# Who copies a chunk's tokens and who adds the halves of its output: a cross-attention and mixture-of-experts kernel

## The reference, cut to what matters

```
x = x + attention(layernorm(x), ctx, ctx)         # x: 2 x 1024 x 256, float32
h = layernorm(x)                                  # 2048 tokens of 256
shared = (silu(h @ sg) * (h @ su)) @ sd           # hidden width 512
logits = h @ gate_w                               # 32 experts
e, top = argmax(logits), max(logits)
xs = h * sigmoid(top)                             # one expert per token
routed = (silu(xs @ G[e]) * (xs @ U[e])) @ D[e]   # G, U: 32 x 256 x 512, D: 32 x 512 x 256
x = x + shared + routed
```

## Time and profile before

| what | value |
|---|---|
| median of 3 runs | 293.36 us (292.28 to 294.63) |
| profiled execution | 291.1 us |
| its span | 289.2 us |
| mean granted clock of TensorE | 0.972 |
| busy: PE, DVE, ACT, POOL | 250.5, 163.1, 94.0, 87.9 us |
| HBM read, written | 59.49 MB, 8.91 MB |

### The profile page before, as it was taken

How to read it: one execution, slowest core, us unless ns; L and a number is a source line. 1 busy time by engine, 2 the same in 40 slices (tenths; PEclk the granted TensorE clock), 3 DMA queues, 4 the chain that set the end, 5 groups by cost and what they waited for, 6 DMA issues and landing times.

```text
span 289.2 us, 12925 instructions
## 1 busy us (share of the span) xinstructions
PE 250.5 (87%) x4627; PEld 184.6 (64%) x4629; DVE 163.1 (56%) x490; ACT 94.0 (33%) x284; POOL 87.9 (30%) x248
## 2 busy tenths in 40 slices
PE   4997899997799899998979999999999999698800
PEld 3765666553375358856867888788788787543700
DVE  0655796878469543016656667666666667424333
ACT  2344875454230110235323333334333333211000
POOL 1262221111005777102222223222222222103772
PEclk9996899999999999999999999999999999999985
DMA  6999994000001325401998869999999999733565
GB/s 196 328 394 410 404 401 157 2 2 1 2 0 37 109 96 165 160 16 50 329 390 286 300 236 331 358 410 415 416 410 411 415 412 409 312 83 94 174 214 164
DMA packets 32559, 68.69 MB, mean 238 GB/s; under 512 B 3966, under 2 KB 18715, under 8 KB 32539
## 3 DMA queue, kind: packets, MB, share of 16 engines
q1 hardware_dynamic: 25723, 61.60, 56.4%
q0 software_dynamic: 1536, 4.20, 4.7%
q10 hardware_dynamic: 5280, 2.62, 3.5%
HBM read 59.49 MB, written 8.91 MB: 237 GB/s over the span
## 4 chain that ended last, share of the span: by engine, by line
PE 66%; DMA 9%; DVE 8%; issue 5%; POOL 5%; ACT 3%; POOLq 1%; SPq 1%; ACTq 1%; DVEq 0%
PE bank L1039 23%; PE bank L961 14%; PE bank L1061 11%; DMA ring_gu<-n_L_ffn_routed_up_w_dram 5%; PE bank L973 5%; POOL xs_flat L463 5%; PE bank L874 3%; PE bank L926 2%; PE bank L909 2%; DMA slot_rows<-late 2%; DVE h_place L531 1%; ACT h_place L749 1%; DVE h_place L532 1%; DMA h_place<-in_L_xattn_kernel_q_dram 1%; DMA xs_flat<-slot_rows,slot_i 1%
## 5 line engine op out<-in xcount | busy, mean ns | idle before, releaser
L1039 PE MATMUL bank<-ring_gu,x_c 128*32 128x128 f32 x2528 | 86.8, 275 | 6.6 <-issue 2.6
L1039 PEld LDWEIGHTS bank<-ring_gu,x_c 128*32 128x32 f32 x2528 | 64.8, 109 | 20.3 <-issue 8.1
L1061 PE MATMUL bank<-ring_d,h_place 128*32 128x128 f32 x1264 | 51.8, 274 | 2.3 <-issue 1.6
L646 DVE TENSOR_TENSOR h_place<-h_place,bank 128x128 f32<-128x128 f32 x79 | 31.2, 395 | 33.2 <-PE bank L1039 30.9
L456 POOL COPY x_c<-xs_flat 128x32 f32 x79 | 16.6, 210 | 101.2 <-PE bank L1039 88.5
L1061 PEld LDWEIGHTS bank<-ring_d,h_place 128*32 128x32 f32 x1264 | 36.1, 109 | 7.7 <-DVE h_place L651 5.3
L792 ACT COPY late<-bank 128x128 f32 (+1 forms) x79 | 21.0, 266 | 57.5 <-PE bank L1061 57.5
L973 PE MATMUL bank<-shd,h_place 128*128 128x256 f32 x128 | 28.4, 380 | 2.1 <-DVE h_place L532 2.1
L651 DVE STREAM_TRANSPOSE h_place<-h_place 128x128 f32<-128x128 f32 x79 | 24.6, 311 | 9.9 <-PE bank L1061 1.7
L787 ACT ACTIVATE h_place<-bank 128x128 f32<-128x128 f32 x79 | 21.9, 277 | 23.6 <-PE bank L1039 19.3
L531 DVE SCALAR_TENSOR_TENSOR h_place<-h_place,bank 128x512 f32<-128x512 f32 x16 | 11.0, 686 | 32.5 <-ACT h_place L749 32.5
(11 more groups left out here) (132 smaller groups left out, 261.9 us busy)
## 6 DMA issues: line engine op xcount, KB each, us to landing
ring_gu<-L_ffn_routed_gate_w_dram SPq DMA_DIRECT2D x32, 512.0 KB, 9.4
ring_gu<-n_L_ffn_routed_up_w_dram SPq DMA_DIRECT2D x32, 512.0 KB, 10.3
ring_d<-L_ffn_routed_down_w_dram SPq DMA_DIRECT2D x32, 512.0 KB, 10.3
slot_rows<-late ACTq DMA_DIRECT2D x10, 256.0 KB, 6.5
x<-in_x_dram SPq DMA_DIRECT2D x4, 512.0 KB, 7.3
slot_rows<-zeros SPq DMA_DIRECT2D x1, 2048.0 KB, 20.4
late<-sorted_rows SPq DMA_DIRECT2D x8, 256.0 KB, 3.4
out_dram<-x SPq DMA_DIRECT2D x8, 256.0 KB, 2.4
```

Of the source, the lines that this page charges most:

```text
L646: v.tensor_tensor(h_r.rearrange("p (m f) -> p m f", m=KF), g_silu.rearrange(rows, m=KF), bank[1][:, 0:P].rearrange(rows, m=KF), ALU.mult). ...
L1039: ins = te.matmul(bank[g][q * LW:(q + 1) * LW, 0:P], x_c[:, k], ring_gu[:, s, g, k, q * P:(q + 1) * P], start=(k == 0), stop=(k == KD - 1))
L1061: ins = te.matmul(bank[2][r:r + LW, 0:DH], hT[:, f * LW:(f + 1) * LW], ring_d[:, s, f, a * DH:(a + 1) * DH], start=(m == 0), stop=(m == HA ...
```

## The change

`take_x` on VectorE takes over the two copies of the next chunk's tokens. In each turn of its loop VectorE first loads the column of chunk c+1, waits for `x0_used`, copies the first half, waits for `u_done`, copies the second half, and only then does the product and the transposition of chunk c. `begin` becomes uint16, and the load has no bounds check. ScalarE takes a down product in two copies of 64 partitions: the lower into `y_all`, the upper into a buffer of its own, `y_second`, at partitions 0 to 63, before which it waits until the sum of the chunk before has been made. GpSimd adds the two. The clearing of `never_early` gets a semaphore, `late_clear`, for ScalarE.

```diff
-        begin = sb("begin", [1, P], I32)
+        begin = sb("begin", [1, P], U16)
+        y_second = sb("y_second", [HR, DH])
...
# GpSimd
-            g_.memset(never_early, 0.0)
-            pool.wait_ge(begin_ready, 1)
-            pool.wait_ge(xsT_ready, NU + 1)
+            g_.memset(never_early, 0.0).then_inc(late_clear, 1)
...
             with pool.Fori(0, n_chunks) as c:
-                col = pool.value_load(begin[0:1, bass.ds(c, 1)], min_val=0, max_val=T)
-                pool.wait_ge(x0_used, c + FREE1)
-                g_.tensor_copy(x_c[:, 0], xsT[:, 0, bass.ds(col, LW)]).then_inc(x0_part, 1)
-                pool.wait_ge(u_done, c + FREE1)
-                g_.tensor_copy(x_c[:, 1], xsT[:, 1, bass.ds(col, LW)]).then_inc(x1_part, 1)
+                pool.wait_ge(y_first, c + 1)
+                pool.wait_ge(y_taken, c + 1 + FREE2)
+                sums = y_all[:, bass.ds(c, 1)].rearrange("p c d -> p (c d)")
+                g_.tensor_tensor(sums, sums, y_second[:], ALU.add).then_inc(y_ready, 1)
...
# VectorE
-            def sum_y(c):
-                dve.wait_ge(y_taken, c + 1 + FREE2)
-                sums = y_all[:, bass.ds(c, 1)].rearrange("p c d -> p (c d)")
-                other = y_halves[HR:P, bass.ds(c, 1)].rearrange("p c d -> p (c d)")
-                v.tensor_tensor(sums, other, sums, ALU.add).then_inc(y_ready, 1)
+            def column(c):
+                return nc.values_load(begin[0:1, bass.ds(c, 1)], engines=(mybir.EngineType.DVE,), min_val=0, max_val=T,
+                                      skip_runtime_bounds_check_because="held to the number of tokens where it is written")
+            def take_x(c, col):
+                dve.wait_ge(x0_used, c + FREE1)
+                v.tensor_copy(x_c[:, 0], xsT[:, 0, bass.ds(col, LW)]).then_inc(x0_part, 1)
+                dve.wait_ge(u_done, c + FREE1)
+                v.tensor_copy(x_c[:, 1], xsT[:, 1, bass.ds(col, LW)]).then_inc(x1_part, 1)
...
             n_chunks = chunk_count(dve)
+            dve.wait_ge(begin_ready, 1)
+            dve.wait_ge(xsT_ready, NU + 1)
+            take_x(0, 0)
             shared_h(3 * KF)
+            take_x(1, column(1))
             gated(0)
             turn_h(0)
+            take_x(2, column(2))
             gated(1)
             dve.wait_ge(down_done, 1)
             turn_h(1)
             with dve.Fori(2, n_chunks) as c:
+                take_x(c + 1, column(c + 1))
                 gated(c)
                 dve.wait_ge(down_done, c)
                 turn_h(c)
-                sum_y(c - 2)
-            sum_y(n_chunks - 2)
-            sum_y(n_chunks - 1)
...
# ScalarE
             def take_y(c):
                 act.wait_ge(down_done, c + 1)
-                a_.copy(y_halves[:, bass.ds(c, 1)].rearrange("p c d -> p (c d)"), bank[2][:, 0:DH]).then_inc(y_taken, 1)
+                a_.copy(y_all[:, bass.ds(c, 1)].rearrange("p c d -> p (c d)"), bank[2][0:HR, 0:DH]).then_inc(y_first, 1)
+                act.wait_ge(y_ready, c + FREE1)
+                a_.copy(y_second[:], bank[2][HR:P, 0:DH]).then_inc(y_taken, 1)
...
             act.wait_ge(zeros_out, 16)
+            act.wait_ge(late_clear, 1)
...
-            act.wait_ge(y_ready, n_chunks)
+            act.wait_ge(y_ready, n_chunks + FREE1)
...
# TensorE
-            for credit in (y_taken, y_taken, silu_done, h_ready, hT_ready, x0_used, u_done):
+            for credit in (y_taken, y_taken, silu_done, h_ready, hT_ready, x0_used, u_done, y_ready):
```

More of the change, by code:

```diff
@@ L270, in build_cross_attention_moe @@
         begin_ready = sem("begin_ready")
+        late_clear = sem("late_clear")
         y_taken = sem("y_taken")
+        y_first = sem("y_first")
         g_done = sem("g_done")
@@ L811, in _ @@
                     if j == 3:
-                        act.wait_ge(y_ready, STORE * b)
+                        act.wait_ge(y_ready, STORE * b + FREE1)
                     if j in (3, 8):
@@ L818, in _ @@
             take_y(n_chunks - 1)
-            act.wait_ge(y_ready, STORE * blocks)
+            act.wait_ge(y_ready, STORE * blocks + FREE1)
             for a in range(HALVES):
                 store_y(blocks - 1, a)
-            act.wait_ge(y_ready, n_chunks)
+            act.wait_ge(y_ready, n_chunks + FREE1)
             for a in range(HALVES):
```

## The result

The changed kernel takes 304.44 us, the median of 4 runs (302.98 to 305.21), against 294.0 us for the kernel before, measured beside it (4 runs, 292.28 to 295.11). The ratio is 1.0397, with a 95% interval of 1.0349 to 1.0444: slower by 4%. I had forecast 316 us, with a range of 303 to 331: the right way and inside the range, but with a loss of 22.5 us where 10.4 were measured. The loss is less than half of the one forecast, and the time lies 1.4 us above the range's lower end. Single executions of a kernel can come out over 1.5% above its fastest ones; all ratios here compare executions without these, the medians are of all executions, and the profiled executions of experiments one and nine were among them.

A forecast was written before the change was run, and what follows sets the result against it. TensorE's instruction order and, close to it, the weights' transfers bound the kernel; VectorE's 1.82 us turn would take over: 78 turns 142.0 plus 1.5 stalls, against 121.8, +21.7; in all +22.5 on 293.4, rounded to 316 us, range 303 to 331.

The forecast's parts named there:

- TensorE's 1.34 us: A chunk's own work on TensorE, about 1.34 us, fitting into VectorE's 1.82 us turn with 0.48 to spare.
- I take 0.20 each: VectorE's two 128x32 copies: a duration plus a 0.02 us gap, 0.20 us each, bounds 0.17 and 0.23.
- The loop's end: VectorE's loop end and jump, from transposition's start to load's start: 0.34 us, bounds 0.30 and 0.38.
- the address work: VectorE's queue from load's end to first copy, with a 46 ns address operation: 0.29 us, bounds 0.24 and 0.48.
- The rival with 0.543 us each time: Every load in VectorE's loop costs 0.543 us, 0.25 more for 78 chunks: 335 us, chance 0.08.
- the stalls that stay: TensorE's loop stalls too long for its spare 0.48 us: 1.1 of one, 0.4 of four others together.
- the end: After the loop, the second copy and slower add stand before the last store: +0.4 us (0.2 to 1.0).
- The load is hidden: In VectorE's turn only the copies count, products 1.56 us apart where short: 297 us, chance 0.06.
- The transfers set the end: The weights' transfers set the loop's end, earlier copies win some 1.5 us: not slower, 292.3 us, chance 0.06.
- GpSimd's sum: GpSimd's 64x128 add takes 0.4 us, between 0.200 and 0.8, beside everything but at the very end.
- TensorE's and the DMA's digits: Sign in the changed kernel's profile: TensorE's and the DMA's busy shares in the loop fall to 7 or 8 tenths.
- TensorE's waits for the first copy: Sign in the loop: TensorE should wait for VectorE's copies, about 0.4 us a chunk.

The follow-up runs named there:

- experiments one: The kernel before with only ScalarE's copy of a down product split in two: 294.95 us, ratio 1.0038.
- nine: The changed kernel with the register load moved ahead of the transposition, plus the product moved ahead of the second copy: 301.36 us, ratio 1.0243.
- the last experiment: The kernel with the load ahead of the transposition, plus GpSimd's sum of chunk c waiting for VectorE's second copy for chunk c+3: 303.21 us, ratio 1.0354.

## Why the prediction was right, and where its size was off

The cause was the one forecast: VectorE's turn becomes one string, its load can't be hidden behind the transposition, and it passes TensorE's 1.34 us. The runs with two loads, no load and an early load show it. The size was off by the terms, product to product (measured in the turn shown above):

| term | priced | measured |
|---|---|---|
| product to transposition | 0.50 | 0.50 |
| transposition to load | 0.34 | 0.40 |
| load | 0.29 | 0.29 |
| load's end to first copy | 0.29 | 0.21 |
| first copy to second | 0.20 | 0.15 |
| second copy to product | 0.20 | 0.13 |
| sum | 1.82 | 1.68 |

- The mis-sized term is "I take 0.20 each" for the two copies, with its bounds 0.17 and 0.23: 0.28 us in place of 0.40, both below the lower bound. I took a duration from a row for a distance between starts. The third copy's run shows that these are different things: with no wait between them, a copy starts 0.09 us behind the one ahead. With the wait for a semaphore and an address in a register, as in the changed kernel, it is 0.15. The kernel before had the sign of it, in GpSimd's timeline where a copy was late and the next had nothing to wait for, two starts 0.15 us apart with 0.21 us of duration, and I didn't use it:

```profile
165.89 0.21 POOL L456 COPY x_c<-xs_flat 128x32 f32 x1 [1.63 <-PE bank L1039]
166.04 0.21 POOL L458 COPY x_c<-xs_flat 128x32 f32 x1
```

- The loop's end was 0.06 us longer than priced, the address work 0.08 shorter: they nearly cancel. Both lie outside their own bounds as well (0.38 at most, 0.24 at least), so four of the six terms did, and the sum stayed inside its 1.66 to 2.13 by 0.02 us only. That the measured time lies in the range is in part luck. The load was right; it was 0.288 us on VectorE. The rival with 0.543 us each time is out, and so, for this load, is the figure of about 600 ns from the Trainium skill's "DMA: Bandwidth & Descriptors", "Latency and other measured facts", that spoke for it: the measurement decides.
- 78 x (1.82 - 1.68) = 10.9 us too much. Against it, the stalls that stay were 133.9 - 78 x 1.68 = 2.9 us, where I had 1.5, and the start and the end took 1.2 us more than forecast. So the profiled execution, 305.2 us, came 8.4 below its 313.6. The rest of the distance from 316 to 304.4 is that I put the median 2.3 us above the profiled execution, as in three runs of the kernel before, and it lay 0.8 below.
- "The load is hidden" is refuted by the two loads. "The transfers set the end" holds for neither the changed kernel, where the last weights land 7.6 us before the last product, nor for the runs with 1.5 us a turn, whose chains have no transfer of weights at the end. The way that the rival of the hidden load named, product, up matmuls, copy, product, is real: it sets the pace once the load is out of the way, at 1.48 us and not 1.56. Its 297 us stand beside the 295.1 and 297.7 measured, but that is in part luck: the backlog of transfers that was to cover its later half isn't in those chains, and 43 of the 78 distances in the kernel before are below 1.45 us, not two thirds.
- Harmless, as forecast: ScalarE's second copy (about 1 us), GpSimd's sum (0.451 us, forecast 0.4), the end (0.6 us more behind the last product, forecast 0.4), the granted clock (1.00 in the loop).
- Of the signs that I had named, two didn't come: products were to be 1.75 to 1.9 us apart, and TensorE's and the DMA's digits were to fall to 7 or 8 tenths. From 181 to 234 us TensorE is busy for 49.67 of 53 us, over 9 tenths, and the DMA share is 0.97.
- TensorE's waits for the first copy were forecast at 0.4 us a chunk; they are 15.8 us in 43 places, 0.37 us each, so 0.2 us a chunk; 10.0 us more in 29 places have no releaser in the profile.

## What to carry to other kernels

Before work moves to an engine, write down that engine's turn as its queue sees it: waits, register loads, address operations and loop end in order, and look at which of them can run beside an instruction that the engine is executing; an engine that was busy two thirds of the time had no room here. A register load belongs ahead of a wait that the queue has to sit out anyway, and moving it there was worth 6 to 7 us of 10. After that the next limit was an instruction that stood between a signal and the work waiting for it: the second copy, behind `u_done` and ahead of the product, cost 0.155 us a turn. Price short independent instructions by the distance between their starts and not by their duration.

## What the runs showed of the hardware

- A VectorE copy of 128x32 (float32, both sides in SBUF) that starts beside GpSimd's sum is held until the sum has ended. In the kernel with the early load 68 first copies that start during a sum take over 0.2 us, up to 0.433, and all end 0.040 to 0.045 us behind the end of that sum; in the run without a load 71 copies and in that with the product first 56 do the same, 0.039 to 0.046 us behind it. The transpositions (0.311 us) beside such a sum are as long as alone: 70 of them overlap one in the last experiment, and so do 76 products, one of whose inputs is in PSUM (0.391 us). The Trainium skill's "SBUF — State Buffer", "SBUF: two separate sides", says that GpSimd and a VectorE instruction in a two-port mode lock a shared pair of ports against each other, for a whole instruction, whichever starts first. For VectorE's copies the trace agrees. The other direction isn't borne out here: of 32 sums that begin while a first copy runs, in the run without a load, none took over 0.492 us against 0.451, though up to 0.182 us of the copy were left. The changed kernel itself hardly meets this, with one long first copy of 79 (0.307 us), since its slow turn keeps the copies behind the sums.
- An instruction on VectorE can start before the one ahead has ended: 0.09 us behind the start of a copy of 0.18, in the run with a third copy.
- A register load takes 0.288 us on VectorE in the median (up to 0.584 in the changed kernel), the same as on TensorE, and two in a row cost twice that.
